# Scan inputs of a Mamba stage from rounded high and low tiles, and sums of eight unpaired slices

## The reference

```python
delta = softplus(dt @ Wdt.T + dt_bias)
def step(state, xs):
    d_t, B_t, C_t, u_t = xs
    dA = exp(d_t[..., None] * A)
    state = dA * state + (d_t * u_t)[..., None] * B_t[:, None, :]
    y_t = einsum('bdn,bn->bd', state, C_t)
    return state, y_t
_, ys = lax.scan(step, init, xs)
y = (swapaxes(ys, 0, 1) + u * D_param) * silu(gate)
return y @ W_out.T
```

## Time and profile before

| | before |
|---|---|
| median of 3 runs | 379.07 us (379.06 to 379.25) |
| profiled execution | 379.14 us, of it the span of the core 377.2 us |
| granted TensorE clock | 1.00 of full speed in all slices |
| busy, PE / DVE / ACT / POOL | 345.2 / 270.6 / 199.3 / 121.4 us |
| the first scan starts, state_sum(28) starts | 86.83 us, 188.27 us |

### The profile page before, as it was taken

The page is one execution under the profiler, slowest core; times in us unless marked ns, Lnnn a source line. Parts: engine busy times, 40 slices in busy tenths (PEclk is TensorE's granted clock), DMA queues, the critical chain, the costliest instruction groups (busy, mean ns, idle before and its releaser), DMA issues.

```text
span 377.2 us, 5167 instructions
## 1 busy us (share of the span) xinstructions
PE 345.2 (92%) x1984; PEld 222.7 (59%) x1984; DVE 270.6 (72%) x355; ACT 199.3 (53%) x397; POOL 121.4 (32%) x96
## 2 busy tenths in 40 slices
PE   0688999999899989999999989899999999899996
PEld 0334444653566656666664877678343477787795
DVE  2776167757887999998967599896820798975381
ACT  1981234179999778597612564563012459251350
POOL 2600000025999889798930011012000020310000
PEclk9999999999999999999999999999999999999999
DMA  6999999563003011156037879699999996000001
GB/s 245 425 420 417 334 422 417 223 223 111 2 1 114 0 36 76 17 225 258 27 115 255 334 301 422 206 349 347 377 423 372 419 420 278 2 2 2 0 2 57
DMA packets 12967, 81.86 MB, mean 217 GB/s; under 512 B 2109, under 2 KB 2365, under 8 KB 3661
## 3 DMA queue, kind: packets, MB, share of 16 engines
q1 hardware_dynamic: 11614, 78.23, 53.2%
q10 hardware_dynamic: 1296, 3.22, 2.3%
q0 software_dynamic: 32, 0.07, 0.0%
HBM read 80.86 MB, written 0.52 MB: 216 GB/s over the span
## 4 chain that ended last, share of the span: by engine, by line
PE 61%; DVE 17%; POOL 9%; DMA 6%; ACT 3%; issue 2%; SPq 0%; DVEq 0%; POOLq 0%; ACTq 0%
PE psum L1027 13%; PE psum L979 8%; PE psum L1249 7%; PE psum L1147 7%; DMA ring<-in_ctx 6%; PE psum L1103 6%; POOL arena L620 4%; PE psum L986 4%; PE psum L1171 4%; PE psum L936 3%; DVE rounded L1654 3%; DVE arena L1611 2%; PE psum L1368 2%; PE psum L1403 2%; POOL plain L620 2%
## 5 line engine op out<-in xcount | busy, mean ns | idle before, releaser
L770 ACT ACTIVATE arena<-arena 128x126 f32<-128x126 f32 x256 | 76.5, 388 | 9.8 <-DVE arena L1611 9.2
L1027 PE MATMUL psum<-ring,hT 128*128 128x512 f32 x128 | 60.6, 602 | 0.8 <-ACT hT L686 0.8
L1611 DVE TENSOR_TENSOR_SCAN arena<-arena,psum 128x1024 f32<-128x1024 f32 x24 | 54.2, 2273 | 3.3 <-PE psum L1103 3.0
L560 POOL TENSOR_TENSOR small<-small 128x1 f32<-128x1 f32 x6 | 9.3, 1543 | 134.6 <-DVE small L1452 129.0
L620 POOL TENSOR_TENSOR arena<-arena 128x1024 f32<-128x1024 f32 x20 | 47.2, 2362 | 5.4 <-DVE arena L1611 5.4
L1654 DVE TENSOR_TENSOR rounded<-ring,rounded 128x2048 fp32r<-128x2048 f32 x16 | 36.5, 2286 | 17.0 <-ACT rounded L797 17.0
L1147 PEld LDWEIGHTS psum<-arena,ident 128*128 128x128 f32 x292 | 35.6, 192 | 12.9 <-issue 10.0
L797 ACT ACTIVATE rounded<-ring 128x2048 fp32r<-128x2048 f32 x16 | 30.6, 1913 | 19.5 <-PE psum L986 11.6
L1027 PEld LDWEIGHTS psum<-ring,hT 128*128 128x128 f32 x128 | 22.2, 190 | 27.1 <-issue 26.0
L1147 PE MATMUL psum<-arena,ident 128*128 128x128 f32 x292 | 37.3, 278 | 0.9 <-POOL arena L623 0.9
L1103 PE MATMUL psum<-plain 64*128 64x512 f32 x128 | 36.1, 641 | 1.7 <-DVE arena L1611 1.4
(11 more groups left out here) (217 smaller groups left out, 577.8 us busy)
## 6 DMA issues: line engine op xcount, KB each, us to landing
ring<-in_w_in SPq DMA_DIRECT2D x16, 1024.0 KB, 14.5
ring<-in_ctx SPq DMA_DIRECT2D x13, 1024.0 KB, 11.3
ring<-in_w_out SPq DMA_DIRECT2D x8, 1024.0 KB, 4.8
ring<-in_ctx_t SPq DMA_DIRECT2D x7, 1024.0 KB, 5.1
ring<-in_w_base SPq DMA_DIRECT2D x4, 1024.0 KB, 4.8
ring<-in_x_wk SPq DMA_DIRECT2D x4, 1024.0 KB, 10.1
ring<-in_a_wo SPq DMA_DIRECT2D x4, 1024.0 KB, 10.9
ring<-in_x_wq SPq DMA_DIRECT2D x3, 1024.0 KB, 8.9
```

Of the source, the lines that this page charges most:

```text
L770: last = act.activation(to, of, ACT.Exp, scale=a_par[:, k, state_no:state_no + 1])
L1027: last = pe.matmul(psum[:, proj_bank(j), :], hT[:, k, :], slot(w_in + u)[:, k % UK, :], start=(k == 0), stop=(k == KT - 1))
L1611: dve.tensor_tensor_scan(state[s % STATES], dA[:, s % 3, :], psum[:, p:p + 2, :].rearrange("p a b -> p (a b)"), 0.0, ALU.mult, ALU.add).th ...
```

## The change

- `scan_input`: `du` and `bdiag` are each kept as a high part, rounded to fp32r, and a low part, the rest. Three pairs, high x high, high x low and low x high, replace the one fp32 product: six matmuls per step in place of two. In fp32r a matmul is one record.
- `bdiag` is made in four VectorE instructions in place of one: a rounding copy and a subtraction of 16 columns, and two products of 1024 columns, each with its own increment of `bdiag_ready`. GpSimd's `cdiag` still waits for the first increment, scan_input(0) for the second.
- `du_copy` on ScalarE writes the high part; a new `du_rest` on VectorE subtracts it from the PSUM bank (512 columns, four times) and signals `du_low`. What waited for `du_copied` on TensorE now waits for `du_low`.
- `DVE_TIMES_C` is empty: GpSimd makes the products with C of steps 0 to 30, VectorE that of step 31 alone.
- There are no pair additions; `state_sum` takes eight slices in every step.
- State buffer 0 moves to the end of `plain`. `high(0)` now waits for 16 scan inputs, `high(1)` no longer waits for `reduced`, and VectorE waits for 29 of `reduced` ahead of `low(0)`.

```diff
-DVE_TIMES_C = (5, 11, 18, 24)
+DVE_TIMES_C = ()
+UNPAIRED = tuple(range(STEPS - DIRECT))
...
-        bdiag = plain[:, 0:NS * L].rearrange("p (n t) -> p n t", n=NS)
-        du = plain[:, NS * L:NS * L + DI]
+        bdiag = carve(rounded, 0, 2, NS, L)
+        du = [carve(rounded, 2 * UN * n, 2, UN) for n in (4, 5, 3, 2)]
+        b_split = carve(rounded, 6 * HN * P, 2, NS)
...
+                    product = pool.tensor_tensor(state[s % STATES], state[s % STATES], c, ALU.mult)
...
+                if s in UNPAIRED:
+                    product.then_inc(pairs_ready, 1)
...
-                act.activation(du[:, UN * g:UN * g + UN], psum[:, 5, :], ACT.Copy).then_inc(du_copied, 1)
+                act.activation(du[g][:, 0, :], psum[:, 5, :], ACT.Copy).then_inc(du_copied, 1)
...
+            act.wait_ge(dbu_ready, 4 * GD)
             high(0)
...
-            act.wait_ge(reduced, STEPS - STATES + 1)
             high(1)
...
                 if g >= 2:
-                    pe.wait_ge(du_copied, g - 1)
+                    pe.wait_ge(du_low, g - 1)
...
-                for b in range(B):
-                    last = pe.matmul(psum[:, input_bank(s, b), :], du[rows_of(b), left], bdiag[rows_of(b), right, :], start=True,
-                                     stop=True)
+                for n, (a, w) in enumerate(((0, 0), (0, 1), (1, 0))):
+                    for b in range(B):
+                        last = pe.matmul(psum[:, input_bank(s, b), :], du[k // GD][rows_of(b), a, left],
+                                         bdiag[rows_of(b), w, right, :], start=(n == 0), stop=(n == 2))
...
-                count = SUMS if paired else HN
+                count = SUMS if paired and s not in UNPAIRED else HN
...
-            dve.tensor_tensor(bdiag, wide(ident2, NS), along(ssm[:, R:R + NS], L), ALU.mult).then_inc(bdiag_ready, 1)
+            step(dve.tensor_copy(b_split[:, 0, :], ssm[:, R:R + NS]))
+            step(dve.tensor_tensor(b_split[:, 1, :], ssm[:, R:R + NS], b_split[:, 0, :].bitcast(F32), ALU.subtract))
+            for w in range(2):
+                dve.tensor_tensor(bdiag[:, w, :, :], wide(ident2, NS), along(b_split[:, w, :].bitcast(F32), L),
+                                  ALU.mult).then_inc(bdiag_ready, 1)
...
+            def du_rest(g):
+                dve.wait_ge(du_copied, g + 1)
+                dve.tensor_tensor(du[g][:, 1, :], psum[:, 5, :], du[g][:, 0, :].bitcast(F32), ALU.subtract).then_inc(du_low, 1)
...
             c_rest_copy(1)
+            du_rest(0)
             c_rest_copy(2)
...
+                if s - 1 in DU_AT:
+                    du_rest(DU_AT.index(s - 1) + 1)
...
+            dve.wait_ge(reduced, STEPS - STATES + 1)
             low(0)
```

More of the change, by code:

```diff
@@ L193, in perceiver @@
         dA = carve(arena, 10336, 3, HN * P)
-        state = [plain[:, 3 * HN * P:4 * HN * P]] + [carve(arena, 13408 + HN * P * i, HN * P) for i in range(STATES - 1)]
+        state = [plain[:, 7 * HN * P:8 * HN * P]] + [carve(arena, 13408 + HN * P * i, HN * P) for i in range(STATES - 1)]
         cdiag = carve(arena, 23296, NS, L)
@@ L324, in perceiver @@
         duT_psum = sem("duT_psum")
+        du_low = sem("du_low")
         du_copied = sem("du_copied")
@@ L618, in _ @@
                     c = cwide[:, HN * P * (s % 2):HN * P * (s % 2) + HN * P]
[L619 to L624, removed]
+                    product = pool.tensor_tensor(state[s % STATES], state[s % STATES], c, ALU.mult)
+                    if s not in UNPAIRED:
+                        products += 1
+                        product.then_inc(prod_ready, 1)
+                        pool.wait_ge(prod_ready, products)
+                if s in UNPAIRED:
+                    product.then_inc(pairs_ready, 1)
+                else:
+                    v = states(s)
+                    pool.tensor_tensor(v[:, :, L * 4:L * 6], v[:, :, L * 4:L * 6], v[:, :, L * 6:L * 8],
+                                       ALU.add).then_inc(pairs_ready, 1)
                 if s == 1:
@@ L1009, in turn @@
                 if j > NG:
[L1011 removed]
+                    pe.wait_ge(du_low, min(j - NG + 2, NG))
                 if j == NB - 1:
@@ L1088, in scan_input @@
                 if s % (2 * GD) == 0:
-                    pe.wait_ge(du_copied, s // (2 * GD) + 1)
+                    pe.wait_ge(du_low, s // (2 * GD) + 1)
                 if s == 0:
-                    pe.wait_ge(bdiag_ready, 1)
+                    pe.wait_ge(bdiag_ready, 2)
                     pe.wait_ge(c_rest, 2)
@@ L1099, in scan_input @@
                 k = s // 2
-                left = slice(P * k, P * k + P)
+                left = slice(P * (k % GD), P * (k % GD) + P)
                 right = slice(HN * (s % 2), HN * (s % 2) + HN)
-                for b in range(B):
-                    last = pe.matmul(psum[:, input_bank(s, b), :], du[rows_of(b), left], bdiag[rows_of(b), right, :], start=True,
-                                     stop=True)
+                for n, (a, w) in enumerate(((0, 0), (0, 1), (1, 0))):
+                    for b in range(B):
+                        last = pe.matmul(psum[:, input_bank(s, b), :], du[k // GD][rows_of(b), a, left],
+                                         bdiag[rows_of(b), w, right, :], start=(n == 0), stop=(n == 2))
                 last.then_inc(dbu_ready, 1)
```

## The result

| | before | after |
|---|---|---|
| median | 379.06 us (4 runs beside the change) | 385.06 us (384.97 to 385.11, 4 runs) |
| ratio to before | | 1.0157, 95% interval 1.0141 to 1.0174 |
| span of the profiled execution | 377.2 us | 383.3 us |
| busy, PE / DVE / ACT / POOL | 345.2 / 270.6 / 199.3 / 121.4 us | 353.2 / 264.6 / 199.9 / 104.6 us |

The change makes the kernel 6.0 us slower.

The account below looks back on a forecast made before the run. TensorE's own work was taken to bound the scan stage. Opening and step 6 +1.4, state sums +11.9, scan inputs -4.0 and idle time -2.8 gave +6.5 us on 379.14: 385.6 us, range 382.7 to 388.2.

Parts of the forecast that it names:

- The bound: Scan stage: TensorE's own work fills it; over some 99 us the other engines cost only 2.8 us of idle time.
- State sums: TensorE, 27 sums of six slices become eight: 1.34 to 1.78 us, +0.44 each, +11.9 us.
- the idle term: TensorE's idle times in the scan stage go as GpSimd and VectorE get slack: -2.8 us, between -2.8 and 0.
- The tally's closing: From scan_input(7) to the output: 96.8 us of blocks plus 2.8 idle make 99.6 against 99.4 us, closing to 0.2.
- Scan inputs: TensorE, six one-pass matmuls replace two fp32 ones: 1.06 to 0.90 us, -0.16 each, -4.0 us for 25.
- The opening and step 6: Split bdiag delays the start by 0.5 us; with time_steps(3)'s wait for du_rest(1), scan_input(7) comes +1.4 us later in all.
- The sum: Whole kernel: +1.4 + 11.9 - 4.0 - 2.8 = +6.5 us, giving 385.6 us.
- A: Rival: a scan input's six one-pass matmuls don't run side by side; block 1.60 us, +17.5, 403 us; chance 0.06.
- B: Rival: fixed parts around a scan input go with its fp32 passes, saving 9.8 us more, 375.8 us; chance 0.07.
- C: Rival: part of the delay is taken up behind the scan stage; half would leave 382.3 us; chance 0.03.
- D: Rival: TensorE still waits, at step 30; the 2.8 us stay, 388.4 us; upper part of the forecast's 0.84.

Follow-up runs that it names:

- six unpaired steps: The full change with pair additions put back in all steps but 1, 9, 16, 21, 28 and 29; 374.91 us, ratio 0.9891.
- slices alone: The kernel before, fp32 scan inputs kept, without pair additions, eight slices per sum, all products but one on GpSimd; 389.05 us, ratio 1.0268.
- the run with the other order: The full change with a scan input's loops exchanged, three one-pass matmuls of batch 0 first, then batch 1's; 385.21 us, ratio 1.0164.
- inputs alone: The full change with all pair additions and VectorE's four products put back, so only scan inputs are split; 383.2 us, ratio 1.0097.
- VectorE's product of step 5 left to GpSimd: The full change with all pair additions and VectorE's products at steps 11, 18 and 24 put back, not step 5; 378.17 us, ratio 0.9992.
- six slices: The full change with sums of six slices but no pair additions, two of eight states left out in steps 0 to 30; 374.15 us, ratio 0.9877.
- du_rest first: Split inputs, all pair additions and VectorE's four products kept, with du_rest queued ahead of VectorE's product with C; 379.40 us, ratio 1.0019.
- four unpaired steps: The full change with pair additions put back in all steps but 1, 12, 27 and 28; 375.80 us, ratio 0.9910.

## Why the prediction was right

**The bound.** That TensorE's own work fills the stage of the kernel before but for some 3 us is borne out: the time followed that work with 10.2 of 10.4 us from the change to six unpaired steps, and the work itself came from a price list of blocks.

**State sums.** Forecast +11.9 us less the idle time. From the earlier trace rows to the chain after, 1.34 became 1.78 us, as forecast. The stretch of "slices alone" is 108.13 - 99.47 = 8.7 us longer, where 11.9 - 2.8 = 9.1 was due. The rest is in the idle term: five waits of the earlier trace rows with 2.8 us of shown idle time cost some 3.2. The ends of matmuls are modelled in the profile, so start times tell more: the sum ahead of the wait of 0.85 us took 2.35 us to the next start, where its like took 1.43 without a wait, so that wait cost 0.92. The tally's closing to 0.2 us was therefore partly luck, with two small errors against each other: the output's 16 matmuls take 2.58 + 2.57 + 8.18 = 13.3 us from start to start, not 13.8. (The row at 188.27 us in the earlier trace rows reads `arena`, so it is state_sum(29); state_sum(28) starts at 185.75. No term hangs on the name.)

**Scan inputs.** Forecast 0.90 us, -4.0 in sum; measured 0.89 to 0.91 and 4.1 in the comparison of stretches. The pace of the one-pass matmuls was that of the fp32r products on 128 rows; in the chain six of them with the block's fixed part take 0.89 to 0.91. "TensorE: Matmul & The Clock Gate" of the Trainium skill, section "Back-to-back issue gap", has the lower price for a single matmul, and the estimate of 0.85 us for the block that was worked out from it was not reached.

**The opening and step 6.** Forecast +0.5 and +1.4 in all, measured +0.3 and +1.4 (108.18 - 106.78). The sum was right and one cause in it was not, so that its size was partly luck: the wait for du_rest(1) stands in the trace, but with it gone only 0.2 us were won. I priced the chain that runs through du_rest and did not price the one beside it, TensorE's own longer sums 1 to 3. From the turn of the first `du` group, which came at 97.26 instead of 96.94, three sums 0.44 longer, two scan inputs 0.16 shorter and the 0.2 of the wait make 106.78 + 0.32 + 1.32 - 0.32 + 0.2 = 108.3; 108.18 was measured. Two paths of nearly one length led to the same place, and I named one.

**The sum.** +6.5 was forecast for the span and +6.1 measured, 385.6 against 385.06 us; most of the 0.4 is the idle times' true size.

**The rivals.** A, that the six matmuls don't run side by side, is out, and the run with the other order shows it is further out than I thought. B is out: the follower of a one-pass block pays 0.19 as before (1.06 for a gate matmul behind a scan input, 0.86 behind a turn; 1.98 against 1.78 for a sum), so the fixed parts don't go with the fp32 passes; that they belong to the change of rows is argued, as no run had blocks without it. C is out: behind the stage the spans differ by what was lost ahead, 171.0 and 171.1 us from the first one-pass product of the output to the end. D did not occur; TensorE's idle time in the stretch is 0.

What the prediction did not see is the faster kernel within the change: split inputs, and long sums in six steps only. Its own sums had it: 4 us of TensorE's work to win with the inputs, and GpSimd at 76 us of 103, with room for most of the additions.

## What to carry to other kernels

When four engines share a stage at 84% to 96% each, tally the engine of the chain block by block, and charge an edit by that engine's prices; what the others are spared is worth only the idle times they cause. Moving work from one near-full engine to another can have its best point between all and nothing: here, of the numbers tried, six of 31 steps, where TensorE waits 0.14 us. In an in-order queue, put the short instruction that another engine waits for ahead of the long one that nobody needs soon; here it started TensorE's next scan input 1.9 us sooner and gained 0.6 us in the end. And before a spread of runs is explained by waits, look at each run's granted clock.

## What the runs showed of the hardware

- Matmuls on the two 64-row halves run side by side in either order of the program that was tried: six of 512 columns took 0.90 us with the batches interleaved and with three of one ahead of three of the other.
- A block of 64-row matmuls among 128-row ones has about 0.20 us of its own beside its passes (1.06 for two fp32 records of 0.43, 0.90 for three one-pass records of 0.233) and makes its follower 0.19 to 0.20 us longer, in the kernel before and in the changed one alike.
- GpSimd's product of 1024 columns beside a VectorE one showed 2.82 us instead of 1.90, VectorE's two 2.36 us together: the one that came second waited.
- Runs of one kernel with split inputs could lie up to 5.5 us apart, in step with the mean granted clock: 379.9 to 380.0 us at 1.00 and 385.2 to 385.5 at 0.987 in "inputs alone", 378.2 and 381.4 (0.996) with VectorE's product of step 5 left to GpSimd, 373.5 and 374.8 (0.995) with six slices. It did not always cost time: with du_rest first, three runs at 0.994 took 379.4 us, as those at 1.00 did, and with four unpaired steps the run at 0.995 was the shortest.
- The one fall of the clock within the stage that a trace shows (du_rest ahead of the product) came right behind 1.83 us in which TensorE stood idle; what decides whether such an idle time brings it is open, since 2.73 us in "inputs alone" did not.
